# A Mamba-style scan with a quantized MLP: products by C on VectorE, and the slots of z, scales, rounding and first copy of h

## The reference

```
state = state * exp(dt * A) + (dt * u) * B
y     = sum over the 16 states of state * C
```

## Time and profile before

| | us |
|---|---|
| runs, median of 3 (lowest to highest) | 657.49 (655.71 to 658.72) |
| profiled execution | 655.74 |
| its span | 653.9 |
| GpSimd busy | 583.1 (89%) |
| VectorE busy | 570.8 (87%) |
| ScalarE busy | 530.1 (81%) |
| TensorE busy | 488.6 (75%) |

### The profile page before, as it was taken

One profiled execution on the slowest core, in us unless ns is written; L12 is line 12 of the kernel. 1 busy time (PEld: TensorE's weight loads), 2 busy tenths in 40 slices (PEclk: granted clock), 3 DMA queues, 4 the chain that ended last, 5 costly groups with the idle time before them and its releaser, 6 DMA issues.

```text
span 653.9 us, 7828 instructions
## 1 busy us (share of the span) xinstructions
PE 488.6 (75%) x2560; PEld 296.4 (45%) x2560; DVE 570.8 (87%) x629; ACT 530.1 (81%) x968; POOL 583.1 (89%) x324
## 2 busy tenths in 40 slices
PE   9797888995563668688566595858676885778987
PEld 3253444553452445455444353545453553445543
DVE  6779769998999899999989989989996989998665
ACT  6763657788999678987898798988899897997675
POOL 1399999997999999999999999999999999999431
PEclk9998889997756979999796889889898898979999
DMA  5698487669970000048420100027610000000001
GB/s 185 206 406 294 167 328 259 228 235 390 384 284 0 32 7 2 24 144 284 152 80 0 33 1 17 2 93 277 244 46 1 17 1 17 0 17 17 2 17 48
DMA packets 24471, 80.76 MB, mean 123 GB/s; under 512 B 2464, under 2 KB 5152, under 8 KB 21360
## 3 DMA queue, kind: packets, MB, share of 16 engines
q1 hardware_dynamic: 24432, 80.27, 33.6%
HBM read 72.53 MB, written 7.73 MB: 123 GB/s over the span
## 4 chain that ended last, share of the span: by engine, by line
POOL 26%; DVE 24%; ACT 16%; PE 14%; issue 13%; DMA 4%; SPq 1%; DVEq 0%; POOLq 0%; ACTq 0%
DVE hh L798 10%; POOL hh L704 7%; POOL hh L837 7%; POOL hh L713 6%; POOL hh L842 5%; ACT da L757 3%; DMA wq<-x 3%; DVE room L1072 2%; DVE da L798 2%; PE bank_b L258 2%; DVE sm L1119 2%; PE bank_y L875 2%; PE bank_t L270 1%; PE bank_a L258 1%; PE da L1251 1%
## 5 line engine op out<-in xcount | busy, mean ns | idle before, releaser
L798 DVE TENSOR_TENSOR_SCAN hh<-da,hh 128x1024 f32<-128x1024 f32 x112 | 254.5, 2280 | 3.3 <-ACT da L764 2.4
L875 PE MATMUL bank_y<-ident,hh 128*128 128x128 f32 x1024 | 147.3, 294 | 17.4 <-POOL hh L842 13.4
L875 PEld LDWEIGHTS bank_y<-ident,hh 128*128 128x128 f32 x1024 | 129.9, 153 | 47.3 <-POOL hh L842 17.1
L842 POOL TENSOR_TENSOR hh<-hh,cc 128x1024 f32<-128x1024 f32 x57 | 134.3, 2356 | 0.2 <-DVE hh L798 0.2
L837 POOL TENSOR_TENSOR hh<-hh,cc 128x1024 f32<-128x1024 f32 x55 | 129.6, 2359 | 0.7 <-ACT hl L788 0.7
L713 POOL TENSOR_TENSOR hh<-pair,bb 128x1024 f32<-128x1024 f32 x30 | 70.6, 2355 | 25.4 <-DMA bb<-xd_scratch 23.8
L713 POOL TENSOR_TENSOR hh<-wq,bb 128x1024 f32<-128x1024 f32 x32 | 75.2, 2357 | 4.4 <-PE bank_y L875 4.4
L704 POOL TENSOR_TENSOR hh<-wq,bb 128x1024 f32<-128x1024 f32 x32 | 75.5, 2359 | 0.7 <-PE bank_y L875 0.7
L704 POOL TENSOR_TENSOR hh<-pair,bb 128x1024 f32<-128x1024 f32 x32 | 75.3, 2358 | 0.0
L764 ACT ACTIVATE da<-pair,cst 128x511 f32<-128x511 f32 x64 | 41.4, 681 | 26.1 <-DVE hh L798 26.1
L757 ACT ACTIVATE da<-wq,cst 128x255 f32<-128x255 f32 x128 | 53.3, 465 | 4.0 <-DVE hh L798 3.9
(11 more groups left out here) (277 smaller groups left out, 1030.6 us busy)
## 6 DMA issues: line engine op xcount, KB each, us to landing
bb<-xd_scratch SPq DMA_DIRECT2D x32, 512.0 KB, 5.4
cc<-xd_scratch SPq DMA_DIRECT2D x32, 512.0 KB, 7.2
wq<-weights SPq DMA_DIRECT2D x12, 1024.0 KB, 6.2
stage<-weights SPq DMA_DIRECT2D x8, 1024.0 KB, 6.2
xin<-x SPq DMA_DIRECT2D x4, 1024.0 KB, 5.4
room<-weights SPq DMA_DIRECT2D x4, 1024.0 KB, 7.7
u_scratch<-wq SPq DMA_DIRECT2D x6, 512.0 KB, 3.0
wq<-x SPq DMA_DIRECT2D x2, 1024.0 KB, 18.4
```

Source lines behind the costliest of these rows:

```text
L798: v.tensor_tensor_scan(to, da, h, 0.0, ALU.mult, ALU.add).then_inc(s_scan, 1)
L842: ins = g_.tensor_tensor(hh[k % NH][:, :, :], hh[k % NH][:, :, :], cc[:, s * GN:(s + 1) * GN, :], ALU.mult)
L875: mm = pe.matmul(bank_y[:, (first + c) * P:(first + c + 1) * P], flat(hh[k % NH])[:, at:at + P], ident[:, :], start=False, stop=(s == STEP ...
```

## The change

VectorE does 19 products by C instead of 16: 47, 59, 79, 85, 97, 109 and 121 are new in its list, 84, 90, 94 and 122 leave it. The power of the mean square and its scaling (`rh`, `rk`) move from t + 6 to t + 5, the scale, rounding and `fin` from t + 7 to t + 6, the first transposes of h and their copy from t + 8 to t + 7, in all engines' lists. z moves one slot later for seven of its sixteen blocks; the slots where it is turned are written out and stay as they were but for the last (119 becomes 118). ScalarE does the copy of the rows' transposes ahead of z where both fall in one slot. Tile 12, whose scale now would fall inside the loop, is kept out of it (END - 1), as it is done after the loop.

```diff
-BY_VECTOR = (14, 16, 25, 45, 49, 53, 62, 67, 68, 73, 77, 84, 90, 94, 115, 122)
+BY_VECTOR = (14, 16, 25, 45, 47, 49, 53, 59, 62, 67, 68, 73, 77, 79, 85, 97, 109, 115, 121)
...
         def z_slot(i):
-            return (26, 28, 30, 31, 36, 42, 48, 54, 68, 74, 80, 86, 98, 104, 110, 117)[i]
+            return (26, 28, 30, 31, 36, 43, 48, 55, 69, 75, 81, 86, 98, 105, 111, 117)[i]
 
         def z_turn_slot(i):
-            b, q = i // NE, i % NE
-            return z_slot(i) + (1 if b == 0 else 2)
+            return (27, 29, 31, 32, 38, 44, 50, 56, 70, 76, 82, 88, 100, 106, 112, 118)[i]
...
                     for i in range(END):
-                        if k == tile_slot(i) + 6:
+                        if k == tile_slot(i) + 5:
                             rh_pool(g_, i)
...
                     for i in range(END - 1):
-                        if k == tile_slot(i) + 8:
+                        if k == tile_slot(i) + 7:
                             hqt_scalar(act, i, 0)
...
-                    for i in range(END):
-                        if k == tile_slot(i) + 7:
+                    for i in range(END - 1):
+                        if k == tile_slot(i) + 6:
                             hq_scalar(act, i, 0)
                             hq_scalar(act, i, 1)
                             fin_scalar(act, i)
...
                     for i in range(END):
-                        if k == tile_slot(i) + 6:
+                        if k == tile_slot(i) + 5:
                             rk_scalar(act, i)
...
+                    for i in range(END + 1):
+                        if k == tile_slot(i) - 1:
+                            xqt_scalar(act, i)
                     for i in TILES:
                         if k == z_slot(i):
                             z_scalar(act, i)
-                    for i in range(END + 1):
-                        if k == tile_slot(i) - 1:
-                            xqt_scalar(act, i)
...
-                    for i in range(END):
-                        if k == tile_slot(i) + 7:
+                    for i in range(END - 1):
+                        if k == tile_slot(i) + 6:
                             scale_vector(v, i)
```

## The result

The changed kernel takes 677.41 us (median of 4 runs, 676.15 to 678.46) against 657.34 us for the kernel before on the same chip: a ratio of 1.0316 with a 95% interval of [1.0284, 1.0348]. The forecast was 666.4 in a range of 651 to 672. The direction is right; the loss is 20 us where 8.9 were priced.

What follows compares the result with a forecast made beforehand. VectorE, with ScalarE's exps and tanhs, was taken to set the pace, with GpSimd catching up but last at the end. Products 3.6, waits 1.9 and rh 3.4 summed to +8.9 us: median 666.4, range 651 to 672.

Steps and rivals of the forecast that it cites:

- rh on GpSimd: After mean square 12, more GpSimd work stands behind rh: end +3.4 us (0 to 5.6); mid-kernel its wait is idle time.
- The rival that priced that tile at 2.2: Slower still: product 97 waits 3 for its rows and tile 100 costs 2.2, +14.1 us, 671.6; chance 0.17.
- Products: Three more products by C on VectorE, taken to set the pace, at 1.2 us each: +3.6 us (0 to 7.2).
- Product 97: First of a new batch, needs rows of C still loading: wait 0 to 3 us, taken as 0.
- The slots: Moved slots of rh, rk, scale, rounding, fin, first copy and z: waits +1.9 us together (-6.8 to +8).
- The tile at 106: Tile without softplus, worked through: about -0.4 us, applied to eight such tiles as -3.2 us.
- the 1.05 us on VectorE: At the tile at 106, VectorE waits 1.05 us for z, which stands behind the copy of the next tile's transposes.
- The sum: Whole kernel: 3.6 + 1.9 + 3.4 = +8.9 us, median forecast 666.4.
- GpSimd is the bound after all: Rival: GpSimd sets the pace, so three products less make the kernel 6.9 us faster, 650.6; chance 0.25.

Runs made afterwards that it cites:

- experiment 5: Kernel before with only rh (GpSimd) and rk (ScalarE) one slot earlier: 670.77 us, ratio 1.0196.
- experiment 9: Kernel before with rh and rk one slot earlier for the nine tiles up to the one at 94, not the last four: 658.92 us, ratio 1.0041.
- experiment 4: Changed kernel with the old list of products by C, all new slots kept: 682.46 us, ratio 1.0399 to the kernel before.
- experiment 11: Changed kernel with rh last in its slot on GpSimd and the old list of products by C: 675.03 us, ratio 1.0277 to the kernel before.
- experiment 13: Changed kernel with rh last in its slot on GpSimd and z at its old slots and order: 664.69 us, ratio 1.013 to the kernel before.
- experiment 3: Kernel before with z at its new slots and behind the copy of the transposes of x; products and rounding as before: 662.93 us, ratio 1.0099.
- experiment 6: Kernel before with rh, rk, scale, rounding, fin and first copy of h one slot earlier, but rh last in its slot on GpSimd: 670.69 us, ratio 1.0188.
- experiment 10: Changed kernel with rh last in its slot on GpSimd, everything else as changed: 667.72 us, ratio 1.0172 to the kernel before.
- experiment 1: Kernel before with the new list of products by C on VectorE alone, slots as before: 656.72 us, ratio 0.9999.
- experiment 12: Kernel before with products 104 and 109 on VectorE too, nothing else: 652.2 us, ratio 0.9939.
- experiment 7: Changed kernel with scale, rounding, fin and first copy of h back at their old slots: 676.85 us, ratio 1.0295 to the kernel before.

## Why the prediction was wrong

The steps, in the order of the prediction:

- *rh on GpSimd, +3.4.* This is the step that failed: "In the middle of the kernel this is idle time of an engine with 6.9 us less to do." The end came as worked out (+3.3 for +3.4), and the wait did too (28.9 us for "10 us or more"). But alone the step costs 13.9 us, and in the changed kernel putting rh late gives 9.7 back. The backlog in the earlier trace rows was read at scans 48 and 91 and the trend carried on to the end. It is no trend: scan 114 starts at 543.39, and its product at 554.86 (shown with experiment 5), so the backlog is 9.2 us there, more than at scan 48. The windows row beside it says the same: from 515.70 to 600 us GpSimd had 0.16 us idle in 84.3, and a wait there is lost time. For the nine tiles up to the one at 94 the sentence nearly holds (2.0 us, experiment 9); the end, which the prediction let begin at mean square 12, begins at the tile at 100. The rival that priced that tile at 2.2 had the right place; rh's wait there grew by 2.7, and with the lateness that GpSimd brought along VectorE lost 3.67.
- *Products, +3.6.* Wrong sign in this kernel. They cost nothing on their own (-0.4) and win 5.0 to 7.3 us beside the earlier rounding (experiments 4 and 11, each against its partner with the new list). The seven new ones (47, 59, 79, 85, 97, 109, 121) follow the scan ahead of a tile's first tanh, and the earlier rounding opens a wait just there (2.25 us at tile 38), so that most of them cost VectorE little, while it keeps the gain of those given back (experiment 13). Products and slots were priced apart, each against the kernel before; they belong together.
- *Product 97, 0 with 3 kept for the range.* The wait is 3.1 us, so 3 was the better value: the rival had it.
- *The slots, +1.9.* Much too small: the slots without rh's wait cost 18.1 us with the old products. The tile at 106, at -0.4, was taken to stand for seven others, and it was the exception: from scan t + 6 to scan t + 12 experiment 11 loses 0.2 us to the kernel before in this tile, but 0.8 to 3.4 in each of the seven (those at 38, 50, 70, 76, 88, 100 and 112), 14.5 together. Of z, the 1.05 us on VectorE was seen, but not that TensorE's turn of z stands ahead of the next tile's products: tanhs wait 8.6 us for TensorE's products in experiment 3 (1.4 in the kernel before). Of the 12.0 us in the changed kernel z's share is not known, as the rounding group makes such waits too (10.6 in experiment 6, with z where it was).
- *The sum.* Going from the kernel before to the changed one over experiments 11 and 10: slots with rh late and old products +18.1, products -7.3, rh's wait +9.7: +20.5, for a measured 20.1. These are steps of one path, so that they add up is no proof; another path gives rh 13.9 and the products -0.4. Of the 11 us that the forecast was short (11.6 on this path), 6.3 are rh's (9.7 for 3.4) and 5.3 those of slots and products together (10.8 for 5.5), and in these two the errors of 16.2 and -10.9 stand against each other.
- *GpSimd is the bound after all (0.25).* True from 515 us on, and not shown before that: three products less spread over the kernel won nothing (experiment 1, in which product 97 also waits 3.3 us for its rows), and two less next to that stretch won 4.8 us (experiment 12). The Trainium skill (Perfetto Trace Analysis, Optimization Strategy) says that a kernel may have several regimes, with another engine most contended in each, and that gaps are to be read within the regime. The runs here agree, with those numbers.

Not settled: why the rounding's place costs only 0.6 us in the changed kernel (experiment 7), since the products by themselves do not hide all of it; and how much of z's cost is TensorE's lower granted clock (0.897 over the span of experiment 3, 0.906 before, 0.873 in the changed kernel) and how much its lateness alone. No run held one of these fixed.

## What to carry to other kernels

Before calling an engine's wait free, look at its busy share in the stretch behind the wait, up to the end of the loop, not at a trend from two points: an engine with 0.16 us idle in 84 cannot make a wait good. Edits that move work between engines and edits that move waits are priced together, place by place: a product put into a wait that another edit opens can cost nothing, where by itself it costs its full time. One tile worked through is no sample when tiles differ in what stands beside them; work each through or bound the sum by the worse.

## What the runs showed that had not been expected

GpSimd's wait for a one-column power reached VectorE some 20 us later (518.37 to 540.11 us in experiment 5), through a queue of products without a gap. And a wait of TensorE can hit the products behind it: after 6.28 us of waiting, with the granted clock at 0.50, the four matmuls of an `a` product took 1.91 us; the next one, at 1.00, took 1.03 (experiment 3).
